# Group norm and displaced 3x3 blur: the first unit's statistics tile by tile, four table words a tile, and loads and stores in another order

## The reference, cut to what matters

```python
x: (16, 768, 64, 64) float32            # offset: (48, 2)
def _gn(v, G=32, eps=1e-5):             # statistics over 24 channels x 64 x 64 of one image
    g = v.reshape(B_, G, C_ // G, H_, W_)
    m = mean(g, axis=(2, 3, 4)); s = var(g, axis=(2, 3, 4))
    return ((g - m) / sqrt(s + eps)).reshape(v.shape)
def _displace(x, offset):               # 48 positions of 16 channels each
    off_px = offset * 64; off_int = round(off_px); sub = off_px - off_int
    shifted = x moved by (off_int[:, 1], off_int[:, 0]) pixels, zero where it leaves the frame
    kern = exp(-(kx*kx + ky*ky) / 0.5), kx = {-1,0,1} + sub_x, ky = {-1,0,1} + sub_y, summed to 1
    return conv 3x3 per channel(shifted, kern, padding='SAME')
return x + _displace(_gn(x), offset)
```

## Time and profile before

| | |
|---|---|
| median of 3 runs | 1061.57 us |
| the profiled execution, its own time | 1058.16 us |
| its span in the profile | 1055.9 us |
| busy: DVE / PE / ACT / POOL | 835.4 / 831.7 / 649.9 / 374.6 us |
| 16 transfer engines, mean share busy | 92.3% |
| moved | 403.08 MB, mean 382 GB/s |

### The profile page before, as it was taken

How to read it: one execution, slowest core, us unless ns; L and a number is a source line. 1 busy time by engine, 2 the same in 40 slices (tenths; PEclk the granted TensorE clock), 3 DMA queues, 4 the chain that set the end, 5 groups by cost and what they waited for, 6 DMA issues and landing times.

```text
span 1055.9 us, 9775 instructions
## 1 busy us (share of the span) xinstructions
PE 831.7 (79%) x2176; PEld 393.1 (37%) x2176; DVE 835.4 (79%) x567; ACT 649.9 (62%) x547; POOL 374.6 (35%) x332
## 2 busy tenths in 40 slices
PE   5985887878888798778789888888987988798710
PEld 2442333334333344333434344434443434344310
DVE  8198797987958788796887969796888969678685
ACT  0675556665567674677566576665655676685761
POOL 3034412634222424243733222332434426324221
PEclk9998898998988899889889989989999889889955
DMA  9827998999999899989999999999999999999937
GB/s 368 350 110 272 416 395 336 423 359 431 376 400 431 322 429 390 406 366 394 421 354 426 423 429 432 429 429 432 429 407 423 377 411 385 402 427 428 390 139 302
DMA packets 27820, 403.08 MB, mean 382 GB/s; under 512 B 3216, under 2 KB 3216, under 8 KB 3216
## 3 DMA queue, kind: packets, MB, share of 16 engines
q1 hardware_dynamic: 27792, 402.71, 92.3%
HBM read 201.38 MB, written 201.33 MB: 381 GB/s over the span
## 4 chain that ended last, share of the span: by engine, by line
DVE 36%; DMA 23%; PE 22%; issue 6%; POOL 5%; ACT 5%; DVEq 2%; ACTq 1%; SPq 0%; POOLq 0%
PE sum_ps L246 19%; DMA xs<-x_dram 19%; DVE xs L527 8%; DVE xs L530 8%; DVE xs L533 7%; DVE smooth L523 6%; DVE smooth L518 6%; DMA out_dram<-xs 4%; ACT frame L320 3%; POOL small L212 2%; POOL small L216 2%; ACTq L298 1%; ACT sum_ps L336 0%; POOL small L224 0%; POOL small L219 0%
## 5 line engine op out<-in xcount | busy, mean ns | idle before, releaser
L246 PE MATMUL sum_ps<-xs,bands 128*128 128x512 f32 x1024 | 505.9, 652 | 49.4 <-DMA xs<-x_dram 49.4
L352 ACT ACTIVATE unused<-xs,small 128x4096 bf16 (+1 forms) x96 | 356.1, 3709 | 17.9 <-ACT small L341 7.6
L246 PEld LDWEIGHTS sum_ps<-xs,bands 128*128 128x128 f32 x1024 | 208.3, 209 | 298.3 <-issue 280.6
L320 ACT ACTIVATE frame<-xs,small (+1 forms) x96 | 223.3, 2327 | 153.5 <-DVE smooth L523 151.9
L246 PE MATMUL sum_ps<-xs,halves 128*128 128x512 f32 x512 | 253.8, 653 | 75.5 <-DMA xs<-x_dram 75.5
L518 DVE SCALAR_TENSOR_TENSOR smooth<-frame,xs 128x1700 f32 (+5 forms) x96 | 163.7, 1705 | 160.3 <-ACT frame L330 104.8
L212 POOL TENSOR_TENSOR small<-small 128x3 f32<-128x3 f32 x32 | 60.2, 1882 | 638.7 <-ACT small L360 638.7
L527 DVE SCALAR_TENSOR_TENSOR xs<-smooth,small,xs 128x1700 f32 (+5 forms) x96 | 163.6, 1704 | 33.4 <-POOL small L224 30.6
L246 PEld LDWEIGHTS sum_ps<-xs,halves 128*128 128x128 f32 x512 | 105.0, 209 | 223.0 <-issue 126.8
L523 DVE SCALAR_TENSOR_TENSOR smooth<-frame,xs,smooth 128x1700 f32<-128x1700 f32 (+5 forms) x96 | 163.5, 1703 | 9.6 <-DVE smooth L518 5.3
L530 DVE SCALAR_TENSOR_TENSOR xs<-smooth,small,xs 128x594 f32 (+9 forms) x96 | 159.8, 1665 | 3.4
(11 more groups left out here) (81 smaller groups left out, 258.5 us busy)
## 6 DMA issues: line engine op xcount, KB each, us to landing
xs<-x_dram SPq DMA_DIRECT2D x96, 2048.0 KB, 14.8
out_dram<-xs SPq DMA_DIRECT2D x96, 2048.0 KB, 13.6
smooth<-offset_dram SPq DMA_DIRECT2D x1, 48.0 KB, 4.1
```

What stands on the lines that cost most here:

```text
L246: last = nc.tensor.matmul(sum_ps[:, :], (FIRST, SAME, SECOND)[i], slot_px(n, c * BANK, (c + 1) * BANK), start=(i == 0 and c == 0), stop=(i ...
L320: nc.scalar.activation(frame[:, bass.ds(b, rows * PITCH)].rearrange("p (r c) -> p r c", c=PITCH)[:, :, LEFT:LEFT + W], xs[:, bass.ds(a, ro ...
L352: nc.scalar.activation(unused[:, :], xs[:, bass.ds(n % SLOTS * PIX, PIX)], ACT.Square, bias=neg_mean[:, i:i + 1], accum_out=squares[:, i:i ...
```

## The change

Four things change together.

1. The start. For unit 0 alone, ScalarE takes each tile's own mean as it lands (`own_means`, an ACTIVATE over 4096 pixels with a running sum) and the squares about that mean (`square_own`), for tiles 0 and 1; VectorE sums tile 2 by a TENSOR_REDUCE. TensorE combines three small columns in place of 24 matmuls of 512 columns, and the spread of the tiles' means is added to the variance (`first_spread`, `first_variances`). Tile 2's squares come after the first frame copy. GpSimd no longer clears the frame; ScalarE zeroes its three borders.
2. The tables are worked out for 48 positions in place of 96 tiles and widened when written.
3. VectorE's loop: four ready words a tile (branch number, target, source, weight column) come by one TENSOR_LOAD into four registers. The packing and unpacking go. The wait on the frame stands in the register instruction ahead of L518's instruction, and the wait on the tile before in the instruction itself; it was the other way round.
4. SyncE's list: within a turn of six tiles the loads follow the stores by a table, `AGAIN`.

The core of the diff:

```diff
             for n in range(TILES):
                 store(n)
-                if 1 <= n <= TILES - SLOTS:
-                    load(n - 1 + SLOTS)
+                for i in AGAIN[n % len(AGAIN)]:      # [(), (0, 1), (), (2,), (3,), (4, 5)]
+                    m = n - n % len(AGAIN) + i + SLOTS
+                    if m < TILES:
+                        load(m)
...
@@ GpSimd
-            V.memset(frame[:, :], 0.0).then_inc(zeros_ready, 1)
+            for s in range(SLOTS):
+                V.memset(slot_of.rearrange("p (n s) -> p n s", s=SLOTS)[:, :, s], float(s * PIX))
+            for i in range(2 * UT):
+                V.memset(word_of[:, :, COLUMN].rearrange("p (u i) -> p u i", i=2 * UT)[:, :, i], 3 * i)
...
@@ TensorE
-            sums(0, range(UT))
-            means(0)
+            first_means()
             for u in range(UNITS):
                 if u + 1 < UNITS:
                     sums(u + 1, range(UT - 1))
-                variances(u)
+                if u:
+                    variances(u)
+                else:
+                    first_variances()
...
@@ ScalarE
+            def own_means(i):
+                act.wait_ge(loaded[i], 16)
+                if i:
+                    act.wait_ge(squares_ready, i)
+                nc.scalar.activation(unused[:, :], slot_px(i), ACT.Copy, scale=-1.0 / PIX,
+                                     accum_out=own_mean[:, i:i + 1]).then_inc(scalar_own_ready, 1)
...
+            own_means(0)
+            act.wait_ge(exp_args_ready, 1)
+            nc.scalar.activation(e[:, :, :, :], e[:, :, :, :], ACT.Exp, scale=-2.0).then_inc(exps_ready, 1)
+            square_own(0)
+            own_means(1)
+            square_own(1)
             act.reg_mov(slot, 0)
+            act.wait_ge(fills_ready, 1)
             load_fill(0)
-            sum_means(0)
-            means(0)
-            means_to_fill(0)
-            for i in range(UT):
-                square(0, i, first=(i == 0))
+            first_means()
+            for i in range(2):
+                first_spread(i)
+            act.wait_ge(border_zero, 3)
             unit_of(0, large=True, first=True)
...
@@ VectorE
+            dve.wait_ge(loaded[UT - 1], 16)
+            V.tensor_reduce(own_sum, slot_px(UT - 1), mybir.AxisListType.X, ALU.add).then_inc(vector_sum_ready, 1)
...
-                dve.wait_ge(tile_done, done)
+                dve.wait_ge(frame_ready, done)
                 V.scalar_tensor_tensor(sm, frame_window(-1), side_w[:, bass.ds(n, 1), 0], frame_window(0),
                                        ALU.mult, ALU.add
-                                       ).wait_op(frame_ready, done_count, "sem-ge").then_inc(half_smooth, 1)
+                                       ).wait_op(tile_done, done_count, "sem-ge").then_inc(half_smooth, 1)
-                dve.reg_load(entry, windows[0:1, bass.ds(done, 1)])
+                dve.reg_load(next_tile, words[0:1, bass.ds(done * WORDS, WORDS)])
...
-                word = dve.snap(entry, min_val=0, max_val=(len(SIDES) ** 2 << FROM_BITS + TO_BITS) - 1)
-                kind_of = dve.snap(word >> FROM_BITS + TO_BITS)
-                base = dve.snap(slot, min_val=0, max_val=(SLOTS - 1) * PIX)
-                dve.reg_mov(to_pixel, base + ((word >> FROM_BITS) & (1 << TO_BITS) - 1))
-                dve.reg_mov(from_pixel, word & (1 << FROM_BITS) - 1)
-                dve.reg_mov(slot, (base + PIX) % (SLOTS * PIX))
+                kind_of = dve.snap(next_tile[KIND], min_val=0, max_val=len(SIDES) ** 2 - 1)
+                dst = dve.snap(next_tile[TO], min_val=0, max_val=SLOTS * PIX)
+                src = dve.snap(next_tile[FROM], min_val=1, max_val=FRAME_ROWS * PITCH)
```

More of the change, by code:

```diff
@@ L81, in build @@
         halves = sb("halves", [P, 2, BIND, IMAGES])
-        small = sb("small", [P, 45])
+        small = sb("small", [P, 53])
         zeros = small[:, 0:1]
@@ L92, in build @@
         col_flat = small[:, 27:45]
+        own_mean = small[:, 45:48]
+        own_sum = small[:, 48:49]
+        mean_64 = small[:, 49:51]
+        spread = small[:, 51:53]
         col_w = col_flat.rearrange("p (u k) -> p u k", k=3)
@@ L239, in sums @@
             def sums(u, tiles):
-                if u and 0 in tiles:
-                    pe.wait_ge(mean_sum_ready, u)
+                if u >= 2 and 0 in tiles:
+                    pe.wait_ge(mean_sum_ready, u - 1)
                 for i in tiles:
@@ L258, in means, with first_means @@
                 nc.tensor.matmul(mean_ps[:, 2:3], OF_SECOND, mean_sum, start=True, stop=True).then_inc(mean_ps_ready, 1)
+            def first_means():
+                first, middle, last = (own_mean[:, i:i + 1] for i in range(UT))
+                pe.wait_ge(scalar_own_ready, 1)
+                nc.tensor.matmul(var_ps[:, 0, 0:1], ALL, first, start=True, stop=False)
+                nc.tensor.matmul(var_ps[:, 1, 0:1], FIRST, first, start=True, stop=False)
+                pe.wait_ge(scalar_own_ready, 2)
+                nc.tensor.matmul(var_ps[:, 0, 0:1], OF_FIRST, middle, start=False, stop=True)
+                nc.tensor.matmul(var_ps[:, 1, 0:1], SAME, middle, start=False, stop=False)
+                nc.tensor.matmul(var_ps[:, 2, 0:1], OF_SECOND, middle, start=True, stop=False)
+                pe.wait_ge(vector_own_ready, 1)
+                nc.tensor.matmul(var_ps[:, 1, 0:1], SECOND, last, start=False, stop=True)
+                nc.tensor.matmul(var_ps[:, 2, 0:1], ALL, last, start=False, stop=True).then_inc(own_ps_ready, 1)
@@ L287, in _ @@
         def _(act):
[L288 to L291, removed]
+            act.wait_ge(constants_ready, 1)
+            left = frame_v[:, PAD:PAD + H, 0:LEFT]
+            above = frame[:, 0:PAD * PITCH]
+            below = frame[:, (PAD + H) * PITCH:]
+            for border in (left, above, below):
+                nc.scalar.activation(border, zeros.unsqueeze(1).to_broadcast(border.shape) if border is left
+                                     else zeros.to_broadcast(border.shape), ACT.Copy).then_inc(border_zero, 1)
             entry = act.alloc_register("entry")
@@ L365, in unit_of @@
                 fill_frame(u, 0)
+                if first:
+                    square(u, UT - 1)
                 variances(u, first)
@@ L419, in _, with by_tile, for_halves @@
             dve.wait_ge(offset_loaded, 16)
-            for u, (at, _half) in enumerate(ORDER):
-                last = V.tensor_copy(off[:, u * UT:(u + 1) * UT, :], given[:, at * UT:(at + 1) * UT, :])
+            for b, at in enumerate(block for pair in PAIRS for block in pair):
+                last = V.tensor_copy(off[:, b * UT:(b + 1) * UT, :], given[:, at * UT:(at + 1) * UT, :])
             chained(last)
+            def by_tile(table):
+                return table.rearrange("p (j h t) -> p j h t", h=HALVES, t=2 * UT)
+            def for_halves(column):
+                return column.rearrange("p (j t) -> p j t", t=2 * UT).unsqueeze(2).to_broadcast(
+                    [P, len(PAIRS), HALVES, 2 * UT])
             FAR, ROUNDER = 1024.0, 1.5 * 2.0 ** 23
@@ L461, in _ @@
                                            ALU.mult, ALU.add))
-            chained(V.scalar_tensor_tensor(fills[:, :], kind[:, :, 1], float(1 << EDGE_BITS + ROW_BITS),
+            chained(V.scalar_tensor_tensor(edge[:, :, 0], kind[:, :, 1], float(1 << EDGE_BITS + ROW_BITS),
                                            edge[:, :, 0], ALU.mult, ALU.add))
-            KIND, TO, FROM = range(3)
+            chained(V.tensor_copy(by_tile(fills[:, :]), for_halves(edge[:, :, 0])))
+            V.engine_nop().then_inc(fills_ready, 1)
@@ L471, in _ @@
+            chained(V.scalar_tensor_tensor(edge[:, :, 1], start[:, :, 1], float(W), start[:, :, 0],
                                            ALU.mult, ALU.add))
[L472 to L475, removed]
```

121 lines of the change are left out of this document (84 added, 37 removed).

## The result

The changed kernel takes 1043.97 us (median of 4 runs, 1041.73 to 1045.1) against 1061.6: a ratio of 0.9828, 95% interval 0.9803 to 0.9853. It is 18 us faster where 36 were forecast.

The account below looks back on a forecast made before the run. Transfers, busy 92.3% of the span, were taken as the bound, at 431 GB/s. Start -12.3, order -21 + 3, loop -4 and end -1.5 sum to -35.8: from 1061.6 to a forecast 1025 us, range 1012 to 1037 (chance 0.55).

Parts of the forecast that it names:

- The start, 12.3 us: Ahead of 95.3 us: transfers lose 24.3 us in place of 36.6, by VectorE's earlier end and an earlier load.
- load 10: Early load that waited for store 2 though its place was free; issued straight behind load 9 it gives 4.9 us.
- SyncE's order, -21 + 3: Two of six loads per turn move ahead of a store: 21 us gained, 3 charged for added waits (bounds 0 and 15).
- the moved kinds: Loads 6k+10 and 6k+14, moved ahead of stores 6k+2 and 6k+6 in SyncE's queue; about seven thin slices, 3 us each.
- the middle: The span between 95.3 and 993 us, where transfers were reckoned to lose 57 us against 431 GB/s.
- the full stretch: Between 536 and 765 us, where the transfer share is full at 425 GB/s; added waits were expected to lose nothing there.
- The rival on SyncE's wait: Stores delayed up to 5 us a turn make it slower, needing 2.3 us a turn; both slower rivals together 0.06.
- The loop, -4 and -1.5: VectorE gains about 15 us from its new tile loop; 4 us come through in the middle, 1.5 in the last six tiles.
- The four-word load: VectorE's register load of four words: 0.1 to 0.3 us a tile more, about 7 us; slower rival 1079, jointly 0.06.
- the bound "nothing": Lower bound on the extra time of VectorE's load of four words over one; the upper was four times as long.
- The end, -1.5: Last six tiles, which nothing hides: 1.5 us of VectorE's loop gain comes through.
- The middle gives it back: Rival: earlier loads do not make stores earlier, empty time only moves; start and end remain, 1044 us, chance 0.27.

Follow-up runs that it names:

- e1: Changed kernel with SyncE's order of before (each load behind its store, none moved ahead): 1046.24 us, ratio 0.9857 to the kernel before.
- e2: Kernel before with only the changed SyncE list added: 1059.21 us, ratio 0.998.
- e3: Changed kernel with load 6k+10 still ahead of store 6k+2, but load 6k+14 back behind store 6k+6: 1040.86 us, ratio 0.9807.
- e4: Changed kernel with load 6k+14 still ahead of store 6k+6, but load 6k+10 back behind store 6k+2: 1051.62 us, ratio 0.9905.
- e10: Changed kernel, its changed SyncE list kept, with TensorE's sums of units 1 to 31 on each pixel's upper 16 bits: 1021.02 us, ratio 0.9608.
- e12: Changed kernel with every load n+9 put directly behind store n, so SyncE waits for every store's landing: 1314.82 us, ratio 1.2391.
- e5: Kernel before with only VectorE's new loop (four words by one load, two waits exchanged), old start and SyncE list: 1052.10 us, ratio 0.9902.
- e6: e3 with unit 0's variances ahead of tile 4's pixels and third frame copy ahead of unit 1's squares: 1042.96 us, ratio 0.9831.
- e13: Kernel before with the new loop and TensorE's sums on each pixel's upper 16 bits; old start, old SyncE list: 1014.43 us, ratio 0.9575.
- e9: Changed kernel with the old SyncE list and TensorE's sums of units 1 to 31 on each pixel's upper 16 bits: 1004.92 us, ratio 0.9469.
- e15: e9 with unit 0's variances ahead of tile 4's pixels and third frame copy ahead of unit 1's squares: 1004.91 us, ratio 0.9479.

## Why the prediction was wrong, by its steps

- **The start, 12.3 us.** Right where it was read: 12.7 us less lost ahead of 95.3. In it were 7.3 of VectorE's earlier end and 4.9 of load 10. Wrong in taking both as given at the end. Of the first about 5 us arrive (0.9857 against 0.9902); with short sums 11 of 10.8 do. Of the second little can have arrived, for the whole list gives 2 to 3 us.
- **SyncE's order, -21 + 3, and load 10's 4.9.** This is the step that failed: 22.9 us forecast, 2 to 3 measured. That is more than the whole miss; the loop made up for some of it. The gain was there to be had: the loads of the moved kinds stood ready for 55 us before and for less than 1 after, and against e1 the list fills 5.4 us of the start and 9.7 of the middle. The price was wrong. I charged 3 us for the added waits, with 15 as the far end, since "where transfers are full nothing is lost". Stores were held 145 us in place of 15, and the full stretch fell from 430 GB/s (e1) to 408, 11.7 us. That it is the list that does this is shown by e1, e2, e3 and e4; that the waits can outweigh the gain is shown by 15 us lost (e10) and 269 (e12). Why the rate falls at a full share stays open. The rival on SyncE's wait named the mechanism and its place; it asked for 2.3 us a turn, and the missing 20 us over 16 turns are 1.2.
- **The loop, -4 and -1.5.** Right in kind, too small: 10.4 us by e5, not 5.5. "Issue" went from 41.0 us to one wait at the start, more than the 20 forecast. I let through about a third of VectorE's 15 us; two thirds came.
- **The four-word load.** 35 ns more at the shortest. In e5, which has the words and not the list, L523 waits 4.8 us in all for L518, for 5.3 before: the bound "nothing" was the true one. The Trainium skill's 200 ns a register ("Runtime: NRT & Kernel Launch", "Instruction fetch mechanics"), given for loads from HBM, doesn't carry over to words in SBUF: the measurement decides.
- **The end, -1.5.** 1.2 by the stretches.
- **What was left out.** TensorE as a bound. I read its 79% as pipelined and said no more, though its sums were 19% of the chain. Halving them gives 32 us. It fits what became of the start: with full sums about 5 of 7.4 us came through (e1, within the noise of all) and none of 5.7 (e6), with short ones all of 10.8 (e13, e9). It does not explain the list, which with short sums did worse.
- **The rival that had the time.** "The middle gives it back" met 1044, by luck in part. Its stretches are right (start and end 13.9, middle 3), but its terms were 13.8 and 4, and one by one the changes give about 5 (start), 10 (loop) and 3 (list). Nor did the empty time only move: dips were filled, and a full stretch grew thin.

## What to carry to other kernels

A wait on a queue that also issues other work costs by what stands behind it, and full transfer engines don't excuse it: look at GB/s at the same share, not at the share. Count both sides before the change, the time that loads stand ready behind stores and the time that stores will stand ready behind the added waits. Before adding up time regained at several places, find the engines that every piece must still pass; here 5.7 us at the start were worth nothing with full sums (e6), and 10.8 us were worth 11 with short ones (e9). An edit's worth depends on what else is late: the same list was worth +2 to +3 and -15 us. And look in the trace whether a test did what it was to do before reading its time: e15 moved tile 0 by 0.6 us, not by 3.

## What the runs showed of the hardware that was not expected

- The transfer share stays at 1.00 while the rate falls from 430 (e1) to 408 GB/s, for the same 16 engines and sizes; only order and overlap of reads and writes differ. The mechanism inside the transfer engines was not found.
- Sums on a two-byte view with a step of two ran in about half the time: TensorE was busy 438 us in all (e9) for 801 with full pixels (e1), with one pass in place of two, at a mean granted clock of 0.577 for 0.902, and the kernel was 41 us faster all the same.
- Three more registers in one load cost 35 ns, at the shortest (306 to 341) and at the median (328 to 362, e5).
